# Attention with 16 heads and routed experts on one core: the softmax sums divide the pairs' outputs in place of the probabilities

## What is computed

```
xn = layernorm(x)
q = l2norm((layernorm(xn)*norm_g + norm_b) @ Wq) * q_scale;  k, v = split(xn @ Wkv)
k, v = null keys and values in front of k, v;  k = l2norm(k) * k_scale
sim = 8 * q @ k.T - slope[h] * |distance|, masked causally
attn = softmax(sim)
x + (attn @ v, heads side by side) @ Wout + shared_expert(xn) + routed_experts(xn)
```

## Time and profile before

| | us |
|---|---|
| median of 3 runs | 530.21 |
| lowest, highest | 529.77, 532.17 |
| the profiled execution, its own time | 529.1 |
| its span in the trace, first to last instruction | 527.4 |
| start of the first entry, about | 163 |
| one entry, from any marker to the same one in the next | 45.9 |
| scores of head 0 in the last entry to the end | 45.15 |

### The profile page before, as it was taken

One profiled execution on the slowest core, in us unless ns is written; L12 is line 12 of the kernel. 1 busy time (PEld: TensorE's weight loads), 2 busy tenths in 40 slices (PEclk: granted clock), 3 DMA queues, 4 the chain that ended last, 5 costly groups with the idle time before them and its releaser, 6 DMA issues.

```text
span 527.4 us, 11888 instructions
## 1 busy us (share of the span) xinstructions
PE 425.0 (81%) x2857; PEld 310.8 (59%) x2857; DVE 405.1 (77%) x1466; ACT 358.5 (68%) x1092; POOL 328.2 (62%) x492
## 2 busy tenths in 40 slices
PE   0657243999997889979988996998899699899885
PEld 0555121677775667657656764765676476567663
DVE  3854713666652899888988988998898899889885
ACT  1334123566666878968886895888689688768864
POOL 2275778940002789678867957876795887777140
PEclk9999767899999999989998999999899999989999
DMA  7940111222221000000001000000100000010010
...
DMA packets 28159, 21.04 MB, mean 40 GB/s; under 512 B 3512, under 2 KB 25312, under 8 KB 28000
## 3 DMA queue, kind: packets, MB, share of 16 engines
...
q10 hardware_dynamic: 816, 0.03, 0.1%
...
## 4 chain that ended last, share of the span: by engine, by line
POOL 31%; PE 21%; issue 20%; DVE 15%; DMA 5%; ACT 4%; POOLq 1%; SPq 1%; DVEq 1%; ACTq 0%
POOL rnorm L415 6%; POOL slot_x L405 6%; POOL arena_b L495 6%; POOL rpow L418 5%; PE bank L1140 4%; PE bank L930 3%; DVE arena_b L885 3%; DVE arena_b L869 3%; POOL pnull L484 3%; PE bank L932 3%; PE bank L931 3%; DMA arena_b<-in_L_ffn_wu_dram 2%; DMA arena_b<-slot_x 2%; PE bank L1072 2%; DVE ssq L846 2%
## 5 line engine op out<-in xcount | busy, mean ns | idle before, releaser
L649 ACT ACTIVATE arena_b<-arena_b,nmx 128x130 f32<-128x130 f32 (+1 forms) x256 | 115.2, 458 | 29.5 <-DVE nmx L885 20.5
L869 DVE TENSOR_SCALAR arena_b<-arena_b,rden 128x130 f32<-128x130 f32 (+1 forms) x256 | 103.9, 450 | 4.5
L885 DVE CUSTOM_DVE_ANT_0 arena_b<-bank,bias 128x130 f32<-128x130 f32 (+1 forms) x256 | 80.9, 353 | 17.1 <-PE bank L1072 9.3
L1072 PE MATMUL bank<-arena_a 64*128 64x130 f32 (+1 forms) x512 | 59.8, 352 | 23.6 <-DVE nmx L885 22.8
L418 POOL TENSOR_TENSOR rpow<-ssm,mhalf 128x8 f32<-128x8 f32 x32 | 52.7, 1648 | 40.4 <-DVE ssm L850 40.4
L1063 PE MATMUL bank<-ident,arena_b 128*128 128x128 f32 x384 | 67.2, 284 | 7.1 <-DVE arena_b L869 7.1
L431 POOL TENSOR_TENSOR arena_b<-arena_b,rnorm 128x512 f32<-128x512 f32 x64 | 67.1, 1048 | 8.4 <-POOL rnorm L421 3.8
L587 ACT ACTIVATE arena_b<-bank 128x512 f32<-128x512 f32 x64 | 38.2, 597 | 31.3 <-PE bank L932 30.5
L415 POOL TENSOR_TENSOR rnorm<-ssm,mhalf 128x8 f32<-128x8 f32 x32 | 52.4, 1639 | 7.7 <-DVE ssm L850 7.7
L846 DVE TENSOR_REDUCE ssq<-arena_b 128x8 f32<-128x512 f32 x64 | 43.4, 678 | 15.5 <-ACT arena_b L587 15.2
L1072 PEld LDWEIGHTS bank<-arena_a 64*128 64x128 f32 x512 | 33.6, 186 | 36.4 <-DVE nmx L885 30.4
...
## 6 DMA issues: line engine op xcount, KB each, us to landing
...
```

The lines of the kernel that those rows point to most:

```text
L649: sc.activation(prob[:, h % 4, c], sim[h % 2][:, c], ACT.Exp, scale=-1.0, bias=nmx[:, h % HEADS, t:t + 1], accum_out=den[:, h % HEADS, t:t ...
L869: ve.tensor_scalar(pr, pr, rden[:, h % HEADS, t:t + 1], None, ALU.mult).then_inc(g.pn, 1)
L885: ve.tensor_tensor_reduce(out=sim[h % 2][:, c], in0=bank[h % 2][:, c], in1=bias[:, c], scale=-SLOPES[h], scalar=3e38, op0=ALU.add, op1=ALU ...
L1072: ins = te.matmul(bank[half][:, c0:c1], qT[r, h // 2, q0:q0 + P], kT[r, h // 2, 0:c1 - c0], start=True, stop=True)
```

## The change

- DVE's multiplication of `prob` (L869) is gone. Reciprocals are taken once for a pair, for both heads (128x4).
- POOL spreads them: `rwide`, 128 x 256, holds for each token and query tile the reciprocal of the even head 64 times and of the odd head 64 times. POOL multiplies the null columns with `rden` as it copies them (`pnull`), and both now stand ahead of the norms in the slot.
- PE transposes `rwide` of the pair before into the fourth 128 columns of banks 2 and 3 (`turned`), so the copies to `probT` have 512 columns; `probT` is double now. The transpositions of a head stand at the end of slot h+2, and no longer in the front part of slot h+3.
- DVE makes `oT` as one float32 product of `opair` and those columns. ACT's L629 is gone. The output product is one plain float32 matmul (`wo`, 128 x 256) in slot h+7; wo_hi and wo_lo are gone, and the transfer of Wout lands in `wo` directly.
- The order on DVE inside a slot is new: reciprocal, scores, side jobs, copy, `oT`.
- "yt" moves from job slot 7 to 9 and yT's copy on ACT to the end of slot 7. `slot_now`, `w_now` and the gathers go to slots 11 to 14, one gather in each, behind the norms. The drain has 11 slots in place of 9.

```diff
-wo = [sb("wo_hi", [P, PAIRS, DIM], F32R), sb("wo_lo", [P, PAIRS, DIM], F32R)]
+wo = sb("wo", [P, PAIRS, DIM])
...
-probT = [sb(f"probT{i}", [P, 3 * P]) for i in range(2)]
+probT = sb("probT", [P, 2, 2, 4 * P])
...
-oT = [[carve_r(SEQ), carve_r(SEQ)] for _ in range(2)]
+oT = [sb(f"oT{i}", [P, SEQ]) for i in range(2)]
+rwide = [sb(f"rwide{i}", [P, SEQ]) for i in range(2)]
...
+def turned(part, s, lag):
+
+    h = head_at(part, s, lag)
+    if part == "first" and h in (0, 1):
+        return h, slice(0, 3 * P)
+    if part == "drain" and s - lag in (0, 1):
+        return s - lag, slice(3 * P, 4 * P)
+    return h, slice(0, 4 * P)
...
             h = head_at(part, s, 2)
-            for _, job_b, job in (behind(part, b, s, 1) if part != "ahead" else []):
-                norms(job_b, job)
-                scale_by_norm(job_b, job)
             if h is not None and h % 2:
                 p = h // 2
-                pool.wait_ge(g.pn, TB * (HEADS * b + h + 1))
+                pool.wait_ge(g.rd, PAIRS * b + p + 1)
+                if part != "first" or p >= 2:
+                    pool.wait_ge(g.ptps, HEADS * b + 2 * p)
+                settled(pool)
+                gp.tensor_copy(rwide[p % 2][:].rearrange("p (t h d) -> p t h d", t=TB, d=DH),
+                               rden[:, 2 * (p % PAIRS):2 * (p % PAIRS) + 2, :].rearrange("p h t -> p t h").unsqueeze(3)
+                               .to_broadcast([P, TB, 2, DH])).then_inc(g.rw, 1)
                 if p == 0 and part != "first":
                     pool.wait_ge(g.pn_hi, 2 * b)
                 settled(pool)
                 q = p % PAIRS
                 two = prob[:, h % 4 - 1:h % 4 + 1, :]
                 for t, c0 in ((0, 0), (1, K0)):
-                    gp.tensor_copy(pnull[:, t, 4 * q:4 * q + 4].rearrange("p (h n) -> p h n", n=2),
-                                   two[:, :, c0:c0 + NNULL]).then_inc(g.pnc, 1)
-            if s == 10 and "own" in whose:
+                    gp.tensor_tensor(pnull[:, t, 4 * q:4 * q + 4].rearrange("p (h n) -> p h n", n=2),
+                                     two[:, :, c0:c0 + NNULL], bc(rden[:, 2 * q:2 * q + 2, t], NNULL),
+                                     ALU.mult).then_inc(g.pnc, 1)
+            for _, job_b, job in (behind(part, b, s, 1) if part != "ahead" else []):
+                norms(job_b, job)
+                scale_by_norm(job_b, job)
+            if s == 11 and "own" in whose:
                 pool.wait_ge(g.fin, b + 1)
                 settled(pool)
                 gp.tensor_copy(slot_now[:], slot[:, bass.ds(b * TB, TB), :]).then_inc(g.now, 1)
                 gp.tensor_copy(w_now[:], wts[:, bass.ds(b * TB, TB), :]).then_inc(g.now, 1)
                 pool.wait_ge(g.now, 2 * b + 2)
                 settled(pool)
-                for t in range(TB):
-                    for c in range(TOPK):
-                        pool.indirect_dma_start(yg[:, t, c, :], None, yg_dram,
-                                                bass.IndirectOffsetOnAxis(ap=slot_now[:, t, c:c + 1], axis=0)
-                                                ).then_inc(g.gath, 16)
+            if 11 <= s < 11 + TB * TOPK and "own" in whose:
+                t, c = (s - 11) // TOPK, (s - 11) % TOPK
+                pool.indirect_dma_start(yg[:, t, c, :], None, yg_dram,
+                                        bass.IndirectOffsetOnAxis(ap=slot_now[:, t, c:c + 1], axis=0)
+                                        ).then_inc(g.gath, 16)
...
-            h = head_at(part, s, 5)
-            if h is not None and h % 2:
-                p = h // 2
-                act.wait_ge(g.pvd, PAIRS * b + p + 1)
-                if part != "first" or p >= 2:
-                    act.wait_ge(g.oread, PAIRS * b + p - 1)
-                sc.activation(oT[p % 2][0], opair, ACT.Copy).then_inc(g.ohi, 1)
             for job in behind(part, b, s, 1):
                 side_out(*job)
-            h = head_at(part, s, 3)
+            h, cols = turned(part, s, 3)
             if h is not None and h % 2 == 1:
+                p = h // 2
                 act.wait_ge(g.ptps, HEADS * b + h + 1)
-                if part != "first" or h >= 2:
-                    act.wait_ge(g.pvd, PAIRS * b + h // 2)
-                sc.activation(probT[1][:], bank[3][:, 0:3 * P], ACT.Copy).then_inc(g.ptev_a, 1)
-            if s == 6 and "prev" in whose:
-                act.wait_ge(g.oread, PAIRS * b)
-                act.wait_ge(g.fin, b)
-                sc.activation(yT, bank[6][:, 0:SEQ], ACT.Copy).then_inc(g.yev, 1)
+                if part != "first" or p >= 2:
+                    act.wait_ge(g.pvd, PAIRS * b + p - 1)
+                sc.activation(probT[:, p % 2, 1, cols], bank[3][:, cols], ACT.Copy).then_inc(g.ptev_a, 1)
             h = head_at(part, s, 1)
...
         for s in steps:
-            h = head_at(part, s, 5)
+            h = head_at(part, s, 2)
             if h is not None and h % 2:
-                p = h // 2
-                dve.wait_ge(g.ohi, PAIRS * b + p + 1)
-                ve.tensor_tensor(oT[p % 2][1], opair, oT[p % 2][0].bitcast(F32),
-                                 ALU.subtract).then_inc(g.olo, 1)
-            h = head_at(part, s, 2)
-            if h is not None:
                 dve.wait_ge(g.exp, TB * (HEADS * b + h + 1))
-                ve.reciprocal(rden[:, h % HEADS, :], den[:, h % HEADS, :]).then_inc(g.rd, 1)
-                dve.wait_ge(g.rd, HEADS * b + h + 1)
-                for t, c in ((0, slice(0, K0)), (1, slice(K0, KS))):
-                    pr = prob[:, h % 4, c]
-                    ve.tensor_scalar(pr, pr, rden[:, h % HEADS, t:t + 1], None, ALU.mult).then_inc(g.pn, 1)
-            h = head_at(part, s, 3)
-            for job in behind(part, b, s, 1):
-                side_out(*job)
-            if h is not None and h % 2 == 0:
-                dve.wait_ge(g.ptps, HEADS * b + h + 1)
-                if part != "first" or h >= 2:
-                    dve.wait_ge(g.pvd, PAIRS * b + h // 2)
-                ve.tensor_copy(probT[0][:], bank[2][:, 0:3 * P]).then_inc(g.ptev_d, 1)
+                hh = slice((h - 1) % HEADS, (h - 1) % HEADS + 2)
+                ve.reciprocal(rden[:, hh, :], den[:, hh, :]).then_inc(g.rd, 1)
             h = head_at(part, s, 0)
             if h is not None:
                 dve.wait_ge(g.sps, HEADS * b + h + 1)
@@ -885,6 +874,25 @@
                     ve.tensor_tensor_reduce(out=sim[h % 2][:, c], in0=bank[h % 2][:, c], in1=bias[:, c],
                                             scale=-SLOPES[h], scalar=3e38, op0=ALU.add, op1=ALU.min,
                                             accum_out=nmx[:, h, t:t + 1]).then_inc(g.ttr, 1)
+            for job in behind(part, b, s, 1):
+                side_out(*job)
+            h, cols = turned(part, s, 3)
+            if h is not None and h % 2 == 0:
+                p = h // 2
+                dve.wait_ge(g.ptps, HEADS * b + h + 1)
+                if part != "first" or p >= 2:
+                    dve.wait_ge(g.pvd, PAIRS * b + p - 1)
+                ve.tensor_copy(probT[:, p % 2, 0, cols], bank[2][:, cols]).then_inc(g.ptev_d, 1)
+            h = head_at(part, s, 5)
+            if h is not None and h % 2:
+                p = h // 2
+                dve.wait_ge(g.pvd, PAIRS * b + p + 1)
+                dve.wait_ge(g.ptev_a, PAIRS * b + p + 2)
+                dve.wait_ge(g.ptev_d, PAIRS * b + p + 2)
+                if part != "first" or p >= 2:
+                    dve.wait_ge(g.oread, PAIRS * b + p - 1)
+                ve.tensor_tensor(oT[p % 2][:].rearrange("p (t q) -> p t q", q=P), opair.rearrange("p (t q) -> p t q", q=P),
+                                 probT[:, (p + 1) % 2, :, 3 * P:4 * P], ALU.mult).then_inc(g.odone, 1)
...
-            h = head_at(part, s, 6)
+            h = head_at(part, s, 7)
             if h is not None and h % 2:
                 p = h // 2
                 if p == 0 and part != "first":
                     pe.wait_ge(g.yev, b)
-                pe.wait_ge(g.olo, PAIRS * b + p + 1)
-                three(bank[6][:, 0:SEQ], [x[:, p % PAIRS, :] for x in wo], oT[p % 2], p == 0,
-                      p == -1).then_inc(g.oread, 1)
+                pe.wait_ge(g.odone, PAIRS * b + p + 1)
+                te.matmul(bank[6][:, 0:SEQ], wo[:, p % PAIRS, :], oT[p % 2][:], start=p == 0,
+                          stop=p == -1).then_inc(g.oread, 1)
...
+            h, cols = turned(part, s, 2)
+            if h is not None:
+                if part != "first" or h >= 2:
+                    pe.wait_ge(g.ptev_a if h % 2 else g.ptev_d, PAIRS * b + h // 2)
+                if cols.start == 0:
+                    pe.wait_ge(g.exp, TB * (HEADS * b + h + 1))
+                    for k, c in enumerate((NNULL, K0 + NNULL, K0 + NNULL + P)):
+                        ins = te.transpose(bank[2 + h % 2][:, k * P:(k + 1) * P], prob[:, h % 4, c:c + P], ident[:])
+                if cols.stop == 4 * P:
+                    p = h // 2 - 1
```

(4 more changed lines are left out.)

40 lines of the change are left out of this document (16 added, 24 removed), and 2 rows, old and new, of the table JOBS.

## The result

The changed kernel takes 571.89 us (median of 4 runs, 569.55 to 575.22) where the kernel before takes 529.99 beside it (4 runs, 528.86 to 532.17). The ratio is 1.080, with an interval of 1.075 to 1.085. The forecast was 518 us, 505 to 533.

A forecast was written before the change was run, and what follows sets the result against it. A circle through PE, ACT, DVE and POOL was taken to set the 45.9 us entry; 1.4 us less over seven entries (9.8), 0.5 in the last entry and 1.2 in the drain gave 11.5 less: about 518 us, range 505 to 533.

The forecast's parts named there:

- The change part by part: Sum of work per engine: DVE 41.3 to about 26 us an entry, PE 40.1 to 43.1, POOL gaining row copies.
- leg a: PE from its kq job of slot 1 to that of slot 4: 7.94 us before, 7.3 forecast, with 0.78 idle subtracted.
- leg b: From PE's kq job of slot 4 through ACT's square and DVE's sum to POOL's power: 2.7 us, unchanged.
- No wait of L1072 for DVE: Sign that the forecast is right: PE's line L1072 would not wait for DVE.
- rival 2: PE's transposition at slot end waits for POOL's row copy, and the half-clock stretch costs up to 1.8 us; 531 us, chance 0.16.
- The circle's sum: Three legs through PE, ACT, DVE and POOL add up to the entry: 45.90 us before, 44.5 forecast, 1.4 less.
- c: From POOL's power down its list to the next entry's kq job of slot 1 on PE: 35.25 us before, 34.5 forecast.
- the last entry and the drain: End of the kernel: 0.5 us less from the last entry's scores, 1.2 less from the chain of short steps.
- The row copy: POOL's rwide: 0.39 us, 0.45 with registers; 6 of the 8 stand in the list up to the next split, 2.7 us.
- rival 3: The spreading copy is slow on POOL, 1.04 us each, entry 48.4; 546 us, chance 0.13; decides from 0.66 us a copy.
- The float32 output product: PE's one plain float32 product in place of three fp32r: 0.50 us against 0.36, 1.1 us more an entry.
- Rival 1: POOL gets the shared ports back and PE becomes the bound, entry at its floor of 43.1 us; 509 us, chance 0.15.

The follow-up runs named there:

- e16: The changed kernel with DVE's score maxima last in its slot, behind side jobs, copy and the product with the reciprocal rows; 523.39 us, ratio 0.988.
- e17: e16 with the row copy moved from GpSimd to DVE, ahead of its side jobs; 525.56 us, ratio interval 0.988 to 0.994.
- e18: e17 with the tail of the kernel before (output product a slot earlier, job in slot 7, gathers together in slot 10); 523.80 us.

## Why the prediction was wrong

**The step that failed** is the one on DVE in "The change part by part": "DVE falls from 41.3 to about 26 us and is no bound any more." Its figure was some 3 us too low (28.9 in the entry): 15.3 adds up rows that overlap, and in the earlier trace rows L869 covers 13.65 us of that entry. But this is not what failed. The step counted DVE's work and not its order, and so put the new waits at nothing. It never said what stands behind the maxima once they are moved ahead of the side jobs, or who waits for the product moved to the slot's end, though the change shows both moves. The same gap is in leg a ("both waits end at DVE's and ACT's lateness", so their idle was subtracted) and in leg b ("nothing in it was late"). What the runs showed in its place: DVE, relieved, waits 17.8 us of an entry ahead of the maxima, PE idles 5.1 us of it behind the late product, and the entry is 5.1 us longer instead of 1.4 shorter; with the maxima last the same work takes 523 us. "No wait of L1072 for DVE" held, for the wrong reason: PE was held at its product with v instead. The rivals looked for a wait on the new row copy, which did come (rival 2), but was the smaller part: 2.4 of 7.5 us.

**The circle's sum came out in the kernel without that fault, and part of that is luck.** In e16, with all of the change's work, busy time by entry is

```profile
298.96:344.76 45.80, 43.31 (x300) 32.03 (x299) 29.99 (x114) 35.34 (x105) 37.77 (x61) 0.96 0.04 11
344.76:389.49 44.73, 41.82 (x300) 30.75 (x299) 30.29 (x114) 35.02 (x105) 37.75 (x61) 1.00 0.04 12
389.49:434.24 44.75, 41.83 (x300) 30.75 (x299) 30.30 (x114) 35.01 (x105) 37.77 (x62) 1.00 0.04 12
```

The forecast had 44.5. PE's timeline and then GpSimd's give its legs:

```profile
346.11 0.50 PE L938 MATMUL bank<-wq_hi,arena_r 128*128 128x512 f32 x1 [0.42 <-POOL arena_r L458]
...
353.60 0.50 PE L938 MATMUL bank<-wq_hi,arena_r 128*128 128x512 f32 x1
...
390.85 0.50 PE L938 MATMUL bank<-wq_hi,arena_r 128*128 128x512 f32 x1 [0.42 <-POOL arena_r L458]
```

```profile
354.95 0.40 POOL L487 COPY rwide<-rden 128x256 f32<-128x256 f32 x1 [1.81 <-DVE rden L866]
...
356.30 1.64 POOL L427 TENSOR_TENSOR rpow<-ssm,mhalf 128x8 f32<-128x8 f32 x1 [0.64 <-DVE ssm L856]
```

a: 7.49 (forecast 7.3), b: 2.70 (2.7), c: 34.55 (34.5). Sum 44.74.

The total of c fits to 0.05 us, its terms don't. Five row copies stand in it and not six, each puts off what follows by 0.36 to 0.44 and not 0.45: 1.9 us where 2.7 were taken. GpSimd still waits 0.8 us in it for DVE's reciprocals and sums, where the forecast had nothing. The gathers saved about 0.1 and not 0.4, the null columns more than was taken. These errors cancel. Nor does c measure GpSimd's own list, as the forecast had it. The chain that ended last in e16 goes from 356 to 377 us through PE, ScalarE and DVE and only then down GpSimd's list, and with the row copies off that list (e17) c is 34.72. So several engines share the bound, and what the circle gave right is the length and not its cause.

**Why 523 and not 518, had the order been right.** By its own terms the forecast was 518.7. The profiled e16 has a span of 521.9 against 527.4, so 5.5 less where the sum had 11.5.
- The sum multiplied 1.4 by seven entries. The first entry gains nothing: from its input's split to the next it took 42.67 us before and 43.02 in e16, less than the circle either time. Four of the five entries visible after it took 44.70 to 44.75, 1.1 to 1.3 less than before; the fifth took 45.80, only 0.08 less.
- That one entry has a mean granted clock of 0.96 where its neighbours have 1.00, a stretch at 1.2 in place of 2.4 GHz, and is 1.07 us longer. In the kernel before the same cost nothing. It is one entry, but the five each of e17 and e18 all have 1.00 and agree within 0.1 us, so the clock is the likely cause. Rival 2 said that it would show, and put at most 1.8 on it.
- From the last split of an input (434.24) to the end 87.7 us pass, 89.1 before (438.30 to 527.4): 1.4 less, no more than one more entry by the circle gives. The forecast had 1.7 more there, for the last entry and the drain; they gave nothing.
- The stages ahead of the first entry's split lost 0.5 us (165.99 to 166.49).

**The other terms.** The row copy: 0.39 taken, measured

```profile
L487 POOL COPY rwide<-rden x64: 387/396/407, 176.8 to 563.7; 128x256 f32<-128x256 f32 x64
```

so rival 3's price (0.66 and more) is refuted, though its time was the nearest of all: the right side for the wrong reason. The Trainium skill (GPSIMD Engine Reference, section Elementwise — side-by-side cycle accounting), weighed in the prediction, has its 2.6 cycles an element for two inputs. Carried over to this copy of one input they gave an estimate of 0.74. The row has half of it, so the figure doesn't carry over; it doesn't test what the section states for two inputs. The float32 output product: 0.50 taken; its two instructions take 0.59 in the timeline and 0.43 in the chain of waits, where three fp32r products had 0.36. PE's whole growth was put too high: 41.8 us at full clock (e16) against 40.1, 1.7 more instead of 3.0. Rival 1's floor of 43.1 was never reached: the shortest entry of e16 has 44.70, with PE busy 41.8 of it.
